# Four residual graph layers on one core: TensorE's order of score products in the attention stage

## Chip, core and metric

One core of a Trainium2 chip runs one program. The metric is the device time of one execution in microseconds. Before the change three runs took 2996.84, 2997.98 and 2998.29 us, the median is 2997.98.

## The reference

Eight graphs (batches) of 1024 nodes with 256 features pass four layers, each of the form "normalise, relu, layer, add". The layer that this change touches is the second, a masked multi-head attention:

```
h = relu(layernorm(x))
q, k, v = h Wq + bq, h Wk + bk, h Wv + bv      # 8 heads of 32
scores = (q k^T) * 32**-0.5 * (adj + adj)      # [8 heads, 1024, 1024]
attn = softmax(scores, axis=-1)
x = x + (attn v) Wo + bo
```

The others are a gated aggregation, a hypergraph convolution and an attention whose weights are adj * exp(q k^T). Everything is float32.

## The kernel before

All engines run their own instruction stream over the eight batches in turn, and are held together by semaphores alone. The order of work on each engine is written out by hand.

In the attention stage the work is cut into 64 units a batch. A unit u is one tile of 128 queries (u // 8) with one head (u % 8, through the table `ORDER`). A unit passes these steps:

- TensorE, `scores(u)` (L1271): two matmuls, 128 queries against 2 x 512 keys, into PSUM banks 0 and 1 for even units or 2 and 3 for odd ones. It first waits for `zs(b, u - 1)`, that VectorE has read the scores of unit u - 2 out of the same pair of banks.
- VectorE (L805): one pass over the 1024 scores of each row; it multiplies by the adjacency and the scale, writes `Z` and gives the maximum `nm`.
- GpSimd, `negate_max` (L565): changes the sign of the maximum.
- ScalarE (L1040): the exponential in place on `Z`, and the sum of each row.
- TensorE, `transposes(u)` (L1293): eight transposes of 128x128 in two halves, each half into one of three PSUM banks that are used in turn (banks 4 to 6). A half waits until the half three turns before has been copied out.
- ScalarE (L1030) copies the first half out of PSUM, VectorE (L760) the second; for one unit of eight ScalarE copies both.
- TensorE, `weighted_values` (L1321): once for four units, 64 small matmuls with the values.

TensorE's loop goes over steps u. Before the change a step issues, in this order: the output projection of a finished tile where it is due (u % 8 == 6), the scores of unit u + 2, the weighted values where they are due (u % 4 == 3), other projections in the first steps of a batch (`BESIDE`), the transposes of unit u, and `spread_inverses` (L1301, two transposes, u % 8 == 0). In step 0 the transposes come first.

VectorE's loop (L797 and on) has its own order in step u: the pass over the scores of unit u, then small work where it is due (`normalise`, `add_output`, the statistics of the next norm), then `evacuate(u - 2)`, the copy of the second half of unit u - 2. ScalarE's has the exponential of u, then its copies for unit u - 1. GpSimd changes the sign for unit u and then writes a part of `H` for the next layer.

Of the kernel before, what the change touches and what calls it, by code (L numbers as in the profile page):

```python
# [31 lines left out]
def build_program(nc, x_in, adj_in, adjT_in, mask_in, wqkT0, wv0, w1attn, bq1, bk1, bv1, bo1,  # L32
# [12 lines left out]
    UNITS = NT * HEADS  # L45
# [18 lines left out]
    with ctx:  # L64
# [258 lines left out]
        def group_due(u, lag):  # L323
            g, rest = divmod(u - lag, HPG)
            return g if rest == 0 and 0 <= g < NT * GROUPS else None

        def tile_due(u, lag):

            g = group_due(u, lag)
            return g // GROUPS if g is not None and g % GROUPS == GROUPS - 1 else None  # L330
# [61 lines left out]
        def rows(t):  # L392
            return slice(t * P, (t + 1) * P)

        def half(n):
            return slice(n * HALF, (n + 1) * HALF)
# [715 lines left out]
        def _(pe):  # L1112
# [43 lines left out]
            def batch(b):  # L1156
# [35 lines left out]
                def project_kq(n):  # L1192
                    s, w, g = KQ[n]
                    product(ps[:, KQ_BANK[n]], [((Wk1, Wq1)[w][:, c, rows(g)], hT1[:, c, half(s)]) for c in range(DT)]).then_inc(kq_ps.sem, 1)

                def project_v(n):

                    if n == 0:
                        pe.wait_ge(*lasts(b, 4))
                    else:  # L1200
                        pe.wait_ge(*vs(b, n))
                    if n == 2:
                        pe.wait_ge(*lo_s(b, len(KQ)))
                    for i in range(2):
                        mm = product(ps[:, 7, i * D:(i + 1) * D], [(hT1[:, c, rows(2 * n + i)], Wv1[:, c]) for c in range(DT)])
                    mm.then_inc(v_ps.sem, 1)
# [52 lines left out]
                def scores(u):  # L1259
                    t, hd = u // HEADS, ORDER[u % HEADS]  # L1260
                    if u >= 2:
                        pe.wait_ge(*zs(b, u - 1))
                    j = hd % HPG
                    if hd < HPG - 1 and t == 0:
                        for s in range(NH):
                            if j < len(kS_in[s]):
                                pe.wait_ge(*kS_in[s][j](b, 64))
                    if hd < len(qS_in[t // TPH]) and t % TPH == 0:
                        pe.wait_ge(*qS_in[t // TPH][j](b, 64))
                    for s in range(NH):  # L1270
                        mm = pe.matmul(ps[:, 2 * (u % 2) + s], qS[:, hd, rows(t)], kS[:, hd, half(s)], start=True, stop=True)  # L1271
                    mm.then_inc(S_ps.sem, 1)
# [15 lines left out]
                def transposes(u):  # L1288
                    pe.wait_ge(*exps(b, u + 1))
                    for s in range(2):  # L1290
                        wait_bank((u, s))
                        for a in range(NT // 2):
                            mm = pe.transpose(ps[:, turn_bank((u, s)), rows(a)], Z[:, u % ZS, rows(NT // 2 * s + a)], ident[:])  # L1293
                        mm.then_inc(T_ps.sem, 1)

                def spread_inverses(t):

                    pe.wait_ge(*rss(b, t + 1))
                    at, first = sums_at(t)
                    for g in range(GROUPS):  # L1300
                        mm = pe.transpose(ps[:, at, first + P * g:first + P * (g + 1)],  # L1301
                                          rs[:, HPG * g:HPG * (g + 1)].rearrange("p h d -> p (h d)"), ident[:])
                    mm.then_inc(R_ps.sem, 1)

                def weighted_values(g, part):


                    if part == 0:
                        pe.wait_ge(*PT_act(b, by_act(HPG * g + HPG - 1)))
                        pe.wait_ge(*PT_dve(b, by_dve(HPG * g + HPG - 1)))  # L1310
                        t = g // GROUPS
                        if g == 0:
                            pe.wait_ge(*vs(b, NT // 2))
                        if g % GROUPS and t < NT - 1:
                            pe.wait_ge(*Rss(b, t + 1))
                        if g % GROUPS == 0 and t:
                            pe.wait_ge(*ctxs(b, t))
                    for kt in range(sum(PARTS[:part]), sum(PARTS[:part + 1])):
                        for j in range(HPG):
                            hd = ORDER[HPG * (g % GROUPS) + j]  # L1320
                            mm = pe.matmul(ps[HD * j:HD * j + HD, 7, P * (g % GROUPS):P * (g % GROUPS + 1)],  # L1321
                                           v[:, kt, HD * hd:HD * hd + HD], PT(HPG * g + j)[:, kt],
                                           start=(kt == 0), stop=(kt == NT - 1))
                    if part == len(PARTS) - 1:
                        mm.then_inc(pv_ps.sem, 1)

                def project(t):
                    pe.wait_ge(*ctxs(b, t + 1))
                    if t < NT - 1:
                        wait_bank((t, "out"))  # L1330
                    product(ps[:, out_bank(t), 0:D], [(ctxn[:, g], Wo1[:, g]) for g in range(GROUPS)]).then_inc(o_ps.sem, 1)
# [10 lines left out]
                for u in range(STEPS):  # L1342
                    if (t := tile_due(u, PROJECT)) is not None:
                        project(t)
                    if u == 0:
                        transposes(u)
                    if u + 2 < UNITS:
                        scores(u + 2)
                    for part in range(len(PARTS)):
                        if (g := group_due(u, WEIGH + part)) is not None:  # L1350
                            weighted_values(g, part)
                    if u in BESIDE:
                        what, n = BESIDE[u]
                        if what == "v":
                            project_v(n)
                        else:
                            pe.wait_ge(*vs(b, 2))
                            project_kq(n)
                    if 0 < u < UNITS:
                        transposes(u)  # L1360
                    if (t := tile_due(u, SPREAD)) is not None:
                        spread_inverses(t)
# [137 lines left out]
            with pe.Fori(0, B) as b:  # L1500
                batch(b)
# [43 lines left out]
```

## Time and profile before

| | us |
|---|---|
| median of three runs | 2997.98 |
| profiled execution, its own time | 2997.46 |
| its span | 2995.7 |
| TensorE matmul busy | 2931.8 (98%) |
| VectorE busy | 1874.1 (63%) |
| ScalarE busy | 1491.7 (50%) |
| GpSimd busy | 722.8 (24%) |

Busy time is the time in which an engine has an instruction at work. The matmuls overlap each other in their records, so the distance between the starts of two matmuls, not the length of a record, tells what one costs. All times in the rows are counted from the start of the span. An entry in square brackets behind a row is idle time of the engine just before it, and what ended it.

### The profile page before, as it was taken

The numbers are of one execution on the slowest core, as the hardware profiler recorded it, in microseconds if no ns is written. First come the engines' busy times: TensorE is split into PE (matmuls) and PEld (weight loads), VectorE is DVE, ScalarE is ACT, GpSimd is POOL, SyncE is SP. The second block draws the span as 40 slices with busy tenths as digits, with TensorE's granted clock in tenths as the row PEclk, the third lists the DMA queues.
The fourth block names the chain that finished last, engine by engine and source line by source line (L and its number), as shares of the span: only waits on it lengthen the run. The fifth ranks groups of instructions, "written<-read, shape, count | busy, mean of one in ns | idle before, by whom it ended". The sixth has DMA issues, their size and how long they took to land.

```text
span 2995.7 us, 63670 instructions
## 1 busy us (share of the span) xinstructions
PE 2931.8 (98%) x23040; PEld 2369.1 (79%) x23040; DVE 1874.1 (63%) x4154; ACT 1491.7 (50%) x2761; POOL 722.8 (24%) x1305
## 2 busy tenths in 40 slices
PE   7999999999999999999999999999999999999999
PEld 6887788877878778888788886888868888688886
DVE  2798427974278742887428874288643886438863
ACT  1784218833178332883328732387323872238622
POOL 0343003430034201342013420134201341014410
PEclk9999999999999999999999999999999999999999
DMA  5202212022120231202311113111132022220200
GB/s 174 93 2 92 78 72 93 2 92 87 62 93 2 92 108 50 84 22 72 134 37 71 49 49 130 56 53 58 58 112 75 34 75 69 84 81 26 83 8 14
DMA packets 95320, 204.34 MB, mean 68 GB/s; under 512 B 10512, under 2 KB 41616, under 8 KB 94992
## 3 DMA queue, kind: packets, MB, share of 16 engines
q1 hardware_dynamic: 93456, 195.76, 18.0%
q8 instruction: 206, 3.38, 0.5%
q0 software_dynamic: 1536, 4.20, 0.4%
q14 instruction: 122, 1.00, 0.1%
HBM read 136.75 MB, written 8.65 MB: 49 GB/s over the span
## 4 chain that ended last, share of the span: by engine, by line
PE 70%; DVE 12%; issue 10%; POOL 4%; ACT 2%; DVEq 0%; DMA 0%; SPq 0%; POOLq 0%; ACTq 0%
PE ps L1116 40%; PE ps L1293 8%; PE ps L1371 7%; PE ps L1271 4%; PE ps L1443 4%; PE ps L1321 4%; DVE junk L847 3%; POOL H L577 3%; DVE Z L805 2%; DVE stats L628 1%; DVE h L863 1%; DVE dn L856 1%; POOL nm L565 1%; ACT Z L1040 1%; PE ps L1153 1%
## 5 line engine op out<-in xcount | busy, mean ns | idle before, releaser
L805 DVE CUSTOM_DVE_ANT_0 Z<-ps,adjN 128x1024 f32<-128x1024 f32 x512 | 623.7, 1218 | 63.7 <-PE ps L1271 63.7
L1040 ACT ACTIVATE Z<-Z,nm 128x1024 f32<-128x1024 f32 x512 | 587.4, 1147 | 51.8 <-POOL nm L565 51.8
L1293 PE MATMUL ps<-ident,Z 128*128 128x128 f32 x4096 | 546.1, 276 | 20.1 <-ACT Z L1040 17.7
L1293 PEld LDWEIGHTS ps<-ident,Z 128*128 128x128 f32 x4096 | 458.8, 140 | 130.0 <-issue 63.8
L1271 PE MATMUL ps<-kS,qS 128*128 128x512 f32 x1024 | 370.4, 444 | 0.8 <-issue 0.8
L577 POOL TENSOR_SCALAR H<-adjN 128x128 fp32r<-128x128 f32 (+1 forms) x456 | 317.5, 696 | 0.0
L565 POOL TENSOR_TENSOR nm<-nm,minus 128x1 f32<-128x1 f32 x512 | 98.1, 192 | 640.0 <-DVE nm L805 635.4
L1116 PE MATMUL ps<-mh,adjT 128*128 128x256 f32 x1024 | 223.6, 379 | 0.0
L1116 PE MATMUL ps<-v,P 128*128 128x257 f32 x1024 | 223.6, 379 | 0.0
L1116 PE MATMUL ps<-hT,t3T 128*128 128x512 f32 x512 | 221.0, 592 | 0.0
L1116 PEld LDWEIGHTS ps<-v,P 128*128 128x128 f32 x1024 | 193.8, 189 | 31.9 <-issue 3.8
L1116 PEld LDWEIGHTS ps<-mh,adjT 128*128 128x128 f32 x1024 | 193.9, 190 | 26.0
L760 DVE COPY PTa<-ps 128x512 f32<-128x512 f32 x256 | 175.8, 687 | 31.8 <-PE ps L1293 31.8
L1116 PEld LDWEIGHTS ps<-hT,t3T 128*128 128x128 f32 x512 | 97.3, 190 | 119.1 <-issue 118.6
L542 POOL TENSOR_SCALAR ve<-mv 128x4 f32<-128x4 f32 x64 | 12.7, 199 | 733.3 <-DVE mv L633 732.6
L701 DVE CUSTOM_DVE_ANT_0 E<-ps,G 128x256 f32<-128x256 f32 x64 | 27.2, 424 | 245.0 <-PE ps L1116 211.0
L1116 PE MATMUL ps<-W,hT 128*128 128x256 f32 x768 | 176.9, 380 | 0.0
L1030 ACT ACTIVATE PTb<-ps 128x512 f32<-128x512 f32 x256 | 144.3, 589 | 59.5 <-PE ps L1293 59.5
L1030 ACT ACTIVATE PTa<-ps 128x512 f32<-128x512 f32 x256 | 150.8, 589 | 38.9 <-PE ps L1293 38.9
L1271 PEld LDWEIGHTS ps<-kS,qS 128*128 128x128 f32 x1024 | 159.5, 191 | 10.6 <-issue 4.8
L1100 ACT ACTIVATE E<-ps,cj 128x512 f32<-128x512 f32 x128 | 87.9, 687 | 159.6 <-PE ps L1116 159.6
L1116 PEld LDWEIGHTS ps<-W,hT 128*128 128x128 f32 x768 | 142.5, 190 | 22.6
(179 smaller groups left out, 5708.5 us busy)
## 6 DMA issues: line engine op xcount, KB each, us to landing
adjT<-adjT_in SPq DMA_DIRECT2D x8, 4096.0 KB, 13.0
adjN<-adj_in SPq DMA_DIRECT2D x8, 4096.0 KB, 18.0
adjT<-adjT_in SPq DMA_DIRECT2D x8, 2048.0 KB, 7.9
qS<-qhi SPq DMA_DIRECT2D x112, 128.0 KB, 2.1
qS<-qlo SPq DMA_DIRECT2D x112, 128.0 KB, 2.1
adjT<-adjT_in SPq DMA_DIRECT2D x8, 1536.0 KB, 12.0
xn<-x_in SPq DMA_DIRECT2D x8, 1024.0 KB, 5.8
out<-x SPq DMA_DIRECT2D x8, 1024.0 KB, 4.8
```

The costliest lines, as they stand in the source:

```text
L565: pool.tensor_tensor(nm[:, u:u + 1], nm[:, u:u + 1], minus[:], ALU.mult).then_inc(nms.sem, 1)
L577: done = pool.tensor_scalar(H[:, t, of], adjN[:, t, of], 0.0, 0.0, ALU.is_equal, ALU.is_equal)
L760: dve.tensor_copy(PT(u)[:, NT // 2:NT], heads_of(ps[:, bank])).then_inc(PT_dve.sem, 1)
L805: dve.tensor_tensor_reduce(Z[:, u % ZS], ps[:, 2 * (u % 2):2 * (u % 2) + 2].rearrange("p a n -> p (a n)"), adjN[:, u // HEADS], SCORE_SCAL ...
L1030: act.activation(PT(u)[:, first:first + NT // 2], heads_of(ps[:, bank]), ACT.Copy).then_inc(PT_act.sem, 1)
L1040: act.activation(Z[:, u % ZS], Z[:, u % ZS], ACT.Exp, bias=nm[:, u:u + 1], accum_out=sm[:, u:u + 1]).then_inc(exps.sem, 1)
L1116: mm = pe.matmul(dst, lhsT, rhs, start=(i == 0), stop=(i == len(pairs) - 1))
L1271: mm = pe.matmul(ps[:, 2 * (u % 2) + s], qS[:, hd, rows(t)], kS[:, hd, half(s)], start=True, stop=True)
L1293: mm = pe.transpose(ps[:, turn_bank((u, s)), rows(a)], Z[:, u % ZS, rows(NT // 2 * s + a)], ident[:])
L1321: mm = pe.matmul(ps[HD * j:HD * j + HD, 7, P * (g % GROUPS):P * (g % GROUPS + 1)], v[:, kt, HD * hd:HD * hd + HD], PT(HPG * g + j)[:, kt], ...
L1371: mm = pe.matmul(dst(n, i), lhs(n, j, i), rhs(n, j, i), start=(j == 0 and i == 0), stop=(j == NT - 1 and i == 0))
L1443: mm = pe.matmul(ps[:, bank(t), 0:D], HT[:, j, rows(t)], (Vh, Vl)[i][:, j], start=(j == 0 and i == 0), stop=(j == NT - 1 and i == 0))
```

## The change

In step u the scores of unit u + 2 were issued. Now an even step issues those of u + 2 and of u + 3, and an odd step issues none. Nothing else is altered; the waits inside `scores` are the same.

```
-                    if u + 2 < UNITS:
-                        scores(u + 2)
+                    if u % 2 == 0:
+                        for ahead in (u + 2, u + 3):
+                            if ahead < UNITS:
+                                scores(ahead)
```

## Rows read from the trace of the kernel before

**Rows 1.** The page's groups: line, operation, tiles and shapes, count | busy us, mean ns | idle

```profile
L805 DVE CUSTOM_DVE_ANT_0 Z<-ps,adjN 128x1024 f32<-128x1024 f32 x512 | 623.7, 1218 | 63.7 <-PE ps L1271 63.7
```

**Rows 2.** One tile's length, busy us (PE, PEld, DVE, ACT, POOL), clock, DMA

```profile
520.45:537.05 16.60, 16.36 (x217) 13.68 (x216) 15.01 (x28) 14.18 (x27) 7.22 (x18) 1.00 0.00 1
```

**Rows 3.** TensorE's waits in the whole span: total us, how many, longest

```profile
PE ps L1293 <- ACT Z L1040: 17.7, 64, 0.5
```

**Rows 4.** Order of time, TensorE, one tile: start us, length us, engine, line

```profile
520.45 0.71 PE L1271 MATMUL ps<-kS,qS 128*128 128x512 f32 x2
...
521.00 1.03 PE L1293 MATMUL ps<-ident,Z 128*128 128x128 f32 x8
...
521.87 0.38 PE L1301 MATMUL ps<-ident,rs 128*128 128x128 f32 x2
...
522.00 0.71 PE L1271 MATMUL ps<-kS,qS 128*128 128x512 f32 x2
...
522.55 1.04 PE L1293 MATMUL ps<-ident,Z 128*128 128x128 f32 x8
...
523.34 0.71 PE L1271 MATMUL ps<-kS,qS 128*128 128x512 f32 x2
...
524.30 1.09 PE L1293 MATMUL ps<-ident,Z 128*128 128x128 f32 x8 [0.24 <-ACT Z L1040]
...
525.14 0.71 PE L1271 MATMUL ps<-kS,qS 128*128 128x512 f32 x2
...
527.67 1.09 PE L1293 MATMUL ps<-ident,Z 128*128 128x128 f32 x8
...
531.34 1.13 PE L1116 MATMUL ps<-Wo,ctxn 128*128 128x256 f32 x4
...
532.12 0.82 PE L1271 MATMUL ps<-kS,qS 128*128 128x512 f32 x2
...
532.78 1.13 PE L1293 MATMUL ps<-ident,Z 128*128 128x128 f32 x8
...
533.67 0.72 PE L1271 MATMUL ps<-kS,qS 128*128 128x512 f32 x2
```

**Rows 5.** Order of time, other engines, same tile

```profile
521.38 1.23 DVE L805 CUSTOM_DVE_ANT_0 Z<-ps,adjN 128x1024 f32<-128x1024 f32 x1
...
522.53 0.68 DVE L760 COPY PTa<-ps 128x512 f32<-128x512 f32 x1
...
522.70 0.19 POOL L565 TENSOR_TENSOR nm<-nm,minus 128x1 f32<-128x1 f32 x1 [1.83 <-DVE nm L805]
...
523.14 1.21 DVE L805 CUSTOM_DVE_ANT_0 Z<-ps,adjN 128x1024 f32<-128x1024 f32 x1
...
523.98 0.19 ACT L1040 ACTIVATION_READ_ACCUMULATOR Z<-Z,nm 128x1 f32 x1
...
528.80 0.69 DVE L760 COPY PTa<-ps 128x512 f32<-128x512 f32 x1 [0.57 <-PE ps L1293]
```

**Rows 6.** Order of time, TensorE, first tile of a batch

```profile
464.30 1.03 PE L1271 MATMUL ps<-kS,qS 128*128 128x512 f32 x2
...
467.69 1.19 PE L1271 MATMUL ps<-kS,qS 128*128 128x512 f32 x4
...
468.72 1.89 PE L1116 MATMUL ps<-W,hT 128*128 128x256 f32 x8
...
481.76 0.71 PE L1271 MATMUL ps<-kS,qS 128*128 128x512 f32 x2
...
483.02 1.09 PE L1293 MATMUL ps<-ident,Z 128*128 128x128 f32 x8 [0.55 <-ACT Z L1040]
...
483.87 0.71 PE L1271 MATMUL ps<-kS,qS 128*128 128x512 f32 x2
```

**Rows 7.** Order of time, end of the stage: a product that waits for VectorE

```profile
606.10 0.41 DVE L773 TENSOR_TENSOR ctxn<-ps,Rs 128x256 f32<-128x256 f32 x1
...
606.56 1.13 PE L1116 MATMUL ps<-Wo,ctxn 128*128 128x256 f32 x4 [0.60 <-DVE ctxn L773]
```

## The prediction

> **What bounds the kernel now.** I read the costliest groups first [rows 1]: the largest of all is VectorE's pass over the scores (L805), so the diff touches the largest stage, attention. Then the busy times of one tile of that stage, eight units [rows 2]. It takes 16.60 us; TensorE is busy 16.36, VectorE 15.01, ScalarE 14.18, GpSimd 7.22. So TensorE sets the pace, but VectorE is only a tenth behind: an order that makes TensorE wait for VectorE at the wrong place has little to give back. The granted clock is 1.00 there. Third, the waits by pairs [rows 3]: the only regular wait of TensorE in the loop is that of the transposes for the exponential, 64 times (8 a batch), 17.7 us in all. Fourth, the order of time of one tile [rows 4] and of the other engines beside it [rows 5]. There the loop can be followed: scores, VectorE, GpSimd's sign, ScalarE's exponential, transposes.
>
> I number the units of a tile 0 to 7 (u mod 8) and write S2 for the two score matmuls of unit 2, z2 for VectorE's pass over them, T2 for its eight transposes, c0 for VectorE's copy of half of T0. Step s is where Ts is issued. In the tile of [rows 4], S2 stands at 520.45, T0 at 521.00, the two small transposes of `spread_inverses` at 521.87, S3 at 522.00, T1 at 522.55, S4 at 523.34, T2 at 524.30, S5 at 525.14. The group of weighted values (W) follows in steps 3 and 7, the output projection in step 6.
>
> Prices on TensorE, start to start [rows 4]: S then T 0.55; T then S 0.79 (522.55 to 523.34); T then another transpose 0.87 (521.00 to 521.87); `spread_inverses` then S 0.13. T2 should follow S4 after 0.55, at 523.89, and starts at 524.30: 0.41 late. It then takes 0.84 instead of 0.79 to the next S, so waiting costs 0.05 more: 0.46 a tile. T6 starts on time (532.78 after S at 532.12; the pair behind the projection takes 0.66 in place of 0.55) but takes 0.89 instead of 0.79, 0.10 more, since it meets ScalarE's two late copies. These are the stalls a reordering can win.
>
> **The change, part by part.** No instruction is added or removed; no DMA, VectorE, ScalarE or GpSimd queue is changed. Each S with an odd number is issued one step earlier: S3 before T0, S5 before T2, S7 before T4, S9 before T6. It is moved past one T, past `spread_inverses` in step 0, and with S9 past the place between projection and W. Four cases.
>
> (a) The matmuls by themselves. At the start of a batch two units stand in a row already: from 467.69 the four score matmuls take until 468.72, 1.03 for two units [rows 6]. So S S T T costs 1.03 + 0.87 + 0.79 = 2.69 where S T S T costs 2 x (0.55 + 0.79) = 2.68. Nothing is gained or lost. Where the order beside W changes, S T S W becomes S S T W with the same kinds of border; I take 0, and 0.05 a tile to either side for the range.
>
> (b) The wait that is removed. S5 now stands between S4 and T2 and fills T2's wait: 0.46 less a tile, if S5 itself is free to go. T6 gets S9 ahead of it and comes 0.55 later than the copies it waited for: 0.10 less.
>
> (c) The wait that is added. S(n) must wait until z(n-2) has read the bank pair. S3 needs z1, S5 needs z3, S7 needs z5, S9 needs z7. Behind the waiting S5, TensorE holds T2, W and T3, which are ready; nothing else on it may pass. Its new time is built from S2 = 0:
> T0 at 1.03; `spread_inverses` at 1.90; T1 at 1.90 + 0.13 + 0.08 (the difference of 0.87 and 0.79, a transpose follows and no S) = 2.11; S4 at 2.90; S5 could start at 3.45 and T2 at 2.90 + 1.03 = 3.93.
> VectorE: z2 starts 0.93 after S2 (520.45 to 521.38) [rows 4, 5]. c0 comes 1.15 after z2, at 2.08, but has to have T0, whose record ends 1.03 after its start, and 0.04 for the hand-over (527.67 + 1.09 = 528.76, copy at 528.80): 1.03 + 1.03 + 0.04 = 2.10. z3 starts 0.61 after c0 (522.53 to 523.14), at 2.71. GpSimd, which is released by the same instruction, starts 1.32 after z does (521.38 to 522.70) [rows 5]. From the end of z (1.23) TensorE needs 0.05 if it behaves as it does for `ctxn` (606.51 to 606.56) [rows 7], or 0.13 as for the exponential (524.17 to 524.30) [rows 4, 5]. The ends are 1.28 and 1.36; I take 1.32, the row of the same releaser. S5 then starts at 2.71 + 1.32 = 4.03, 0.58 after it could. The pair behind the projection costs 0.66 to the next T; a pair behind a wait lacks a weight load ahead of time in the same way, so I take 0.66. T2 starts at 4.69 in place of 3.93: 0.76 more a tile. Bounds: 0.55 for the pair and 1.28 give T2 at 4.54, 0.61 more. The slowest pair of the trace has a record of 1.03 where the usual one has 0.71 (464.30 [rows 6] and 520.45 [rows 4]), so 0.87 to the next; with 1.36 that gives 4.94, 1.01 more.
>
> The Trainium skill (TensorE: Matmul & The Clock Gate, Part 2, "Step-by-step: what each phase is for") says that TensorE's queue pulls weight loads ahead of matmuls in flight. If it also pulled S5's load past the wait, the pair would take 0.55 and not 0.66, which takes 0.11 x 56 = 6 us off the sum below. The transposes that waited speak against it: T2 took 0.05 longer behind its wait [rows 4].
>
> (d) The other moved pairs. By the same steps (T's end 1.07 after its start, a copy 0.61, z to S 1.32) S(n) can go 3.00 after the start of the T whose copy stands ahead of z(n-2). S7: 3.00 after T2. Between stand T2 (0.87), W (525.14 to 527.67 less 0.55 for S, 1.98), T3 (0.79) and S6 (0.55), 4.19 in all; free. S9: 3.00 after T4. Between stand T4 and T5 (0.87 each), the projection (531.34 to 532.12, 0.78) and S8 (0.66), 3.18; free by 0.18. S11, the S3 of the next tile: z9 stands behind c6 as well, W and T7 lie between; free. z2 is not held up: T7 starts 0.79 before S2, so c7 can start at 1.07 - 0.79 = 0.28 and is through at 0.89, before z2 at 0.93.
>
> The first tile of a batch is different. In step 0 the old order already has S2, S3 in a row [rows 6]. In step 2 other projections lie beside the loop and no stall arises. In step 6, T6 waits for the exponential until 483.02, then come S9 at 483.87 and W. S8 starts at 481.76, S9 then fits between 482.31 and 483.02: 0.50 less a batch. In step 62, at the end of the batch, there is no S left to put ahead of T62, so nothing is won there.
>
> Sum for a batch: seven tiles lose 0.76 (5.32), seven win 0.46 (3.22), six win 0.10 (0.60), the first tile wins 0.50. 5.32 - 3.22 - 0.60 - 0.50 = +1.00; eight batches +8 us. The profiled execution took 2997.46 (its span is 2995.7), so it goes to 3005.5; from the median of the runs, 2997.98, to 3006.0.
>
> **Rivals.**
> 1. No measurable change. The new wait is at its lower bound, 0.61: 4.27 - 4.32 = -0.05 a batch, 0 in all; up to 0.72 it stays below 0.2%. For it: all terms are differences of a few hundredths, and the one restart of a matmul behind VectorE took only 0.05 [rows 7]. Against it: it needs both the short wake and a pair that restarts without loss. Time 2998 to 3004.
> 2. Faster. The mechanism would be that S5 finds z3 done: then the stalls in (b) are pure gain, -4.32 x 8 = -35 us, 2963. The point from which it decides: z3 has to start 0.58 earlier, which is nearly the 0.61 of c0, the copy between z2 and z3. If VectorE were ahead by one such copy, it would hold. Against it: VectorE's queue is fixed, and both c0 and z3 itself (it writes the `Z` buffer that T0 reads) need T0 to be through. For a win of 6 us the new wait would have to cost below 0.51 a tile, which is under both bounds.
> 3. Clearly slower. The restart costs as much as the pair at 464.30, 1.01 a tile: 7.07 - 4.32 = 2.75, +22 us, 3020. It gets there too if S9 in step 6 waits: its spare 0.18 is small, and 0.2 of waiting in seven tiles and eight batches is 11 us on top of the forecast. For it also: VectorE has only 1.6 us of slack in a tile.
> 4. The change has no effect because the second pair waits until the old place. For S5 it comes close: the old order issues it after T2 (525.14, 4.69 after S2), the new one at 4.03. T2, which once went ahead of it, would then go behind it. If S5 got no earlier than 4.69, T2 would come at 5.35, 1.42 a tile: 9.94 - 4.32 = 5.62 a batch, +45 us, 3043. Against it: the steps of (c) leave nothing for S5 to wait for after 4.03.
>
> **How the numbers follow.** A difference of 0.2% is 6 us, about what can be told from none. Forecast 0.42; rival 1 0.32; rival 2 0.08; rival 3 0.16; rival 4 0.02. The likeliest is the forecast. Slower by over 0.2% has the forecast and rival 3, 0.60 together; the forecast's 8 us lies close to the 6, and 0.06 of it may fall below. So slower 0.54, same 0.38, faster 0.08. Low end: 0 with 0.05 x 56 = 3 us for the borders of (a), 2995. High end: +22 with 3, 3023.
>
> **What would show it.** In the changed profile the pairs of L1271 stand in fours. S5 starts about 4.0 after S2, with an idle or late start released by VectorE's L805, 56 such waits. T2 no longer waits for ScalarE; the regular wait of L1293 for the exponential shrinks from 64 to the first tiles' 8. Tiles take 16.60 + 0.76 - 0.46 - 0.10 = 16.80. All other stages keep their length. The prediction is wrong if S5 does not wait, if S9 or S3 waits, if the tile is under 16.60, or if T1 or T5, which now stand straight behind T0 and T4, wait for the copies of the PSUM banks.

## The result, and the profile after

The changed kernel takes 3015.0 us (median of four runs, 3013.99 to 3016.09), the kernel before 2997.9 in the same comparison: a ratio of 1.0058, 95% interval 1.0045 to 1.0071. That is 17.1 us slower, inside the range of 2995 to 3023 and on the forecast side, but twice the forecast 8.

The page of the changed kernel, busy times first, then the groups that answer to [rows 1] and the matmuls of the loop (busy, mean of one, idle before and what ended it):

```profile
PE 2933.7 (97%) x23040; PEld 2388.5 (79%) x23040; DVE 1883.9 (63%) x4154; ACT 1509.6 (50%) x2761; POOL 722.8 (24%) x1305
...
L805 DVE CUSTOM_DVE_ANT_0 Z<-ps,adjN 128x1024 f32<-128x1024 f32 x512 | 624.0, 1219 | 59.7 <-PE ps L1271 59.7
...
L1293 PE MATMUL ps<-ident,Z 128*128 128x128 f32 x4096 | 535.1, 275 | 3.0 <-ACT PTb L1030 2.3
...
L1271 PE MATMUL ps<-kS,qS 128*128 128x512 f32 x1024 | 328.2, 431 | 31.7 <-DVE nm L805 31.7
```

VectorE's pass is as long as before (1219 ns a piece). The idle time of the transposes for ScalarE, 17.7 us in [rows 3], is gone from their line; the scores have 31.7 us in its place, released by VectorE. The waits of TensorE say how often:

```profile
PE ps L1271 <- DVE nm L805: 31.7, 64, 0.9
```

64 waits for VectorE stand where 64 waits for ScalarE stood. The prediction had 56, one in each tile but the first. So each batch has one more. It is the long one, of 0.9 us: without it (the first experiment below, where the first tile has the old order) 56 waits of together 24.5 us are left.

One tile of the changed kernel, columns as in [rows 2]:

```profile
508.32:525.07 16.75, 16.31 (x218) 14.05 (x216) 15.20 (x28) 14.48 (x27) 7.21 (x18) 1.00 0.01 3
```

The tile went from 16.60 to 16.75 us; 16.80 was forecast. The sum over a batch then shows where the time is. All lengths are medians over the eight batches of one profiled execution. I take the first tile from S0 to T7's start and the others from the last transpose of a tile to that of the next. The first tile went from 24.46 to 25.42, +0.96 (in the batch whose rows are shown, from 461.94 to 486.40 before and from 465.27 to 490.69 after). Tiles 1 to 6 went from 16.60 to 16.76, +0.16 each. The last went from 16.13 to 16.38, +0.25. The rest of a batch takes 228.52 in both. Together 0.96 + 0.96 + 0.25 = 2.17 a batch, 17.4 us in eight. Single batches differ (one of the eight first tiles of the kernel before took 25.41), and the spans of the two profiled executions are 16.7 us apart. The loss of the later tiles is as forecast; the first tile, which was to win 0.50, lost 0.96.

The changed tile in order of time, the rows that answer to [rows 4, 5]. S2 starts at 508.32:

```profile
508.32 1.17 PE L1271 MATMUL ps<-kS,qS 128*128 128x512 f32 x4
...
509.25 1.23 DVE L805 CUSTOM_DVE_ANT_0 Z<-ps,adjN 128x1024 f32<-128x1024 f32 x1
509.33 1.03 PE L1293 MATMUL ps<-ident,Z 128*128 128x128 f32 x8
...
510.42 1.04 PE L1293 MATMUL ps<-ident,Z 128*128 128x128 f32 x8
510.49 0.69 DVE L760 COPY PTa<-ps 128x512 f32<-128x512 f32 x1
510.57 0.19 POOL L565 TENSOR_TENSOR nm<-nm,minus 128x1 f32<-128x1 f32 x1 [1.74 <-DVE nm L805]
...
511.10 1.22 DVE L805 CUSTOM_DVE_ANT_0 Z<-ps,adjN 128x1024 f32<-128x1024 f32 x1
...
511.21 0.72 PE L1271 MATMUL ps<-kS,qS 128*128 128x512 f32 x2
...
512.37 0.73 PE L1271 MATMUL ps<-kS,qS 128*128 128x512 f32 x2 [0.44 <-DVE nm L805]
...
512.94 1.03 PE L1293 MATMUL ps<-ident,Z 128*128 128x128 f32 x8
...
516.64 1.19 PE L1271 MATMUL ps<-kS,qS 128*128 128x512 f32 x4
...
517.67 2.02 PE L1293 MATMUL ps<-ident,Z 128*128 128x128 f32 x16
...
519.53 1.09 PE L1116 MATMUL ps<-Wo,ctxn 128*128 128x256 f32 x4
...
520.27 1.03 PE L1271 MATMUL ps<-kS,qS 128*128 128x512 f32 x3
```

S2 and S3 stand in one group, T0 follows at 1.01 (forecast 1.03), T1 at 2.10 (2.11), S4 at 2.89 (2.90). z2 is at 0.93. The copy c0 comes at 2.17 (2.10) and z3 at 2.78 (2.71). c0 has to have T0, whose record ends at 1.01 + 1.03 = 2.04; the copy starts 0.13 behind that end, where the forecast had 0.04. S5 starts at 512.37, 4.05 after S2 (4.03), and 1.27 after z3: a wait of 1.16 - 0.55 = 0.61 behind S4. T2 follows S5 after only 0.57 (0.66), at 4.62 (4.69), and does not wait for ScalarE.

In the row at 520.27 (S8 and S9) the fourth matmul lies outside the window of this view.

The new wait in the first tile of a batch. This is the stretch from the end of step 2 to T4:

```profile
476.07 1.14 ACT L1040 ACTIVATE Z<-Z,nm 128x1024 f32<-128x1024 f32 x1
...
477.49 0.69 ACT L990 ACTIVATE qhi<-ps,bq1c 128x512 fp32r<-128x512 f32 x1 [0.18 <-PE ps L1116]
...
478.21 0.75 DVE L745 SCALAR_TENSOR_TENSOR qlo<-ps,bq1c,qhi 128x512 fp32r<-128x512 f32 x1 [1.49 <-ACT qhi L990]
...
478.88 0.68 DVE L760 COPY PTa<-ps 128x512 f32<-128x512 f32 x1
...
479.13 0.71 PE L1271 MATMUL ps<-kS,qS 128*128 128x512 f32 x2
479.48 1.22 DVE L805 CUSTOM_DVE_ANT_0 Z<-ps,adjN 128x1024 f32<-128x1024 f32 x1
...
480.75 0.30 PEld L1271 LDWEIGHTS ps<-kS,qS 128*128 128x128 f32 x2 [1.34 <-DVE nm L805]
480.75 0.73 PE L1271 MATMUL ps<-kS,qS 128*128 128x512 f32 x2 [0.91 <-DVE nm L805]
...
481.32 1.89 PE L1116 MATMUL ps<-W,hT 128*128 128x256 f32 x8
...
483.04 1.04 PE L1293 MATMUL ps<-ident,Z 128*128 128x128 f32 x8
```

The projection of step 2 is followed by ScalarE's `qhi` (L990) and by VectorE's `lower_kq` (L745) that reads it. `qhi` stands behind an exponential, but that was over when it started; its row names the projection (L1116) as what it waited for. Behind `lower_kq` on VectorE stand c2 and z5. So z5 starts at 479.48, when S6 has already been issued, and S7 can start only 1.27 later, at 480.75, 1.62 after S6 instead of 0.55. Behind S7 TensorE holds the projection of the values at 481.32 and T4 at 483.04.

The same stretch of the kernel before:

```profile
474.60 0.75 DVE L745 SCALAR_TENSOR_TENSOR qlo<-ps,bq1c,qhi 128x512 fp32r<-128x512 f32 x1 [1.20 <-ACT qhi L990]
...
475.63 0.71 PE L1271 MATMUL ps<-kS,qS 128*128 128x512 f32 x2
...
475.86 1.22 DVE L805 CUSTOM_DVE_ANT_0 Z<-ps,adjN 128x1024 f32<-128x1024 f32 x1
```

There too z5 starts behind S6, 0.23 after it, but S7 was issued only after T4, at 478.70, and had nothing to wait for.

### The profile page after: what moved, and what is told of

Its sections match the earlier page's. It is cut to its first block, busy times and chain, and to the rows that moved or that the text cites. A ratio compares the mean times of both kernels' runs of the same rounds, so it can differ in the third digit from the quotient of the medians.

```text
span 3012.4 us, 63670 instructions
## 1 busy us (share of the span) xinstructions
PE 2933.7 (97%) x23040; PEld 2388.5 (79%) x23040; DVE 1883.9 (63%) x4154; ACT 1509.6 (50%) x2761; POOL 722.8 (24%) x1305
## 4 chain that ended last, share of the span: by engine, by line
PE 80%; DVE 11%; issue 5%; ACT 2%; POOL 1%; DVEq 0%; DMA 0%; SPq 0%; POOLq 0%; ACTq 0%
PE ps L1116 40%; PE ps L1293 13%; PE ps L1271 7%; PE ps L1373 7%; PE ps L1321 7%; PE ps L1445 4%; DVE junk L847 3%; DVE stats L628 1%; DVE h L863 1%; DVE dn L856 1%; POOL H L577 1%; PE ps L1153 1%; DVE Z L805 1%; DVE Ul L688 1%; ACT h2T L1072 1%
## 5 line engine op out<-in xcount | busy, mean ns | idle before, releaser
L805 DVE CUSTOM_DVE_ANT_0 Z<-ps,adjN 128x1024 f32<-128x1024 f32 x512 | 624.0, 1219 | 59.7 <-PE ps L1271 59.7
L1293 PE MATMUL ps<-ident,Z 128*128 128x128 f32 x4096 | 535.1, 275 | 3.0 <-ACT PTb L1030 2.3
L1271 PE MATMUL ps<-kS,qS 128*128 128x512 f32 x1024 | 328.2, 431 | 31.7 <-DVE nm L805 31.7
L1271 PEld LDWEIGHTS ps<-kS,qS 128*128 128x128 f32 x1024 | 171.9, 189 | 85.2 <-DVE nm L805 59.7
L1116 PE MATMUL ps<-mh,adjT 128*128 128x256 f32 x1024 | 223.6, 379 | 0.0
L1116 PE MATMUL ps<-v,P 128*128 128x257 f32 x1024 | 223.6, 379 | 0.0
L1116 PE MATMUL ps<-hT,t3T 128*128 128x512 f32 x512 | 221.0, 592 | 0.0
L1116 PEld LDWEIGHTS ps<-v,P 128*128 128x128 f32 x1024 | 193.8, 189 | 31.9 <-issue 3.8
L1116 PEld LDWEIGHTS ps<-mh,adjT 128*128 128x128 f32 x1024 | 193.9, 190 | 26.0
L1116 PEld LDWEIGHTS ps<-hT,t3T 128*128 128x128 f32 x512 | 97.3, 190 | 119.1 <-issue 118.6
L1116 PE MATMUL ps<-W,hT 128*128 128x256 f32 x768 | 177.6, 381 | 0.0
L934 DVE TENSOR_TENSOR P<-E,adjT 128x512 f32<-128x512 f32 x128 | 88.7, 693 | 113.6 <-ACT E L1100 113.6
## 6 DMA issues: line engine op xcount, KB each, us to landing
adjN<-adj_in SPq DMA_DIRECT2D x8, 4096.0 KB, 17.1
```

Source lines behind the costliest of these rows:

```text
L805: dve.tensor_tensor_reduce(Z[:, u % ZS], ps[:, 2 * (u % 2):2 * (u % 2) + 2].rearrange("p a n -> p (a n)"), adjN[:, u // HEADS], SCORE_SCAL ...
L1116: mm = pe.matmul(dst, lhsT, rhs, start=(i == 0), stop=(i == len(pairs) - 1))
```

## The experiments

All are changes of the list of units that a step issues, or of the one constant `BOTH`. Times are medians; the kernel before took 2998.2 us beside the first four, 2996.8 beside the next four and 2997.0 beside the last two. Lengths of tiles are again medians over one profiled execution; "the tile" is one of tiles 1 to 6 of a batch, counted from 0.

**Which tiles lose.** First the old order in the first tile alone, then pairs in the first tile alone.

```
+ for ahead in ((u + 2,) if u < HEADS else ((u + 2, u + 3) if u % 2 == 0 else ())):
```

> Pairs only from step 8 of a batch on; the first tile (steps 0 to 7) keeps the old order. Theory A (the changed kernel's loss is 1.0 us in the first tile and 0.15 us in every later one, because in the first tile S7 waits for z5, which stands behind lower_kq on VectorE): the first tile returns to 19.55 us and the time falls by 8 x 1.0 = 8 us to about 3007, later tiles stay at 16.75. Rival B (the first tile's loss only moves: the wait is met by the next pair): under 3 us gained, 3012 or more.

Measured: 3008.3 us (ratio 1.0035, 1.0021 to 1.0048). The first tile is back at its length of before, later tiles are at 16.76.

```
+ for ahead in (((u + 2, u + 3) if u % 2 == 0 else ()) if u < HEADS else (u + 2,)):
```

> Pairs only in steps 0 to 7 of a batch, the old order in all later tiles. Theory A: first tile 20.5 us, later tiles 16.60 as before the change, time 2998 + 8 = 3006. Rival B: what is lost in the first tile is won back by TensorE's waits behind it, time 2998 to 3001.

Measured: 3004.9 us (1.0023, 1.0014 to 1.0032). The first tile is 0.96 longer than before, all later ones 16.60. So the two losses stand beside each other and add: 10.1 us of the later tiles and 6.7 of the first make 16.8, against 17.1 for the change. Rival B fell in both.

**What fails in the first tile.** One unit is put back, S7:

```
+ for ahead in ((u + 2,) if u in (4, 5) else ((u + 2, u + 3) if u % 2 == 0 else ())):
```

> The changed kernel with one unit put back: the scores of unit 7 are issued in step 5 again, behind T4, all other pairs stay. Theory A: S7's wait is the whole fault of the first tile; without it the first tile is 0.5 us shorter than the old 19.55 (the gain that the prediction had for step 6), so 1.5 us a batch and 12 us in all are won, 3003. Rival C (pairing in the first tile is bad in several places, S5 or S9 too): the first tile stays over 19.8 us and the time over 3008.

Measured: 3005.2 us (1.0023, 1.0014 to 1.0033), ten less than the change. The first tile is 1.28 shorter than with the change and 0.31 shorter than the old one (463.99 to 488.14 from S0 to T7, 24.15 against 24.46). The rows from S6 on:

```profile
477.85 0.71 PE L1271 MATMUL ps<-kS,qS 128*128 128x512 f32 x2
...
478.19 1.22 DVE L805 CUSTOM_DVE_ANT_0 Z<-ps,adjN 128x1024 f32<-128x1024 f32 x1
...
478.40 1.89 PE L1116 MATMUL ps<-W,hT 128*128 128x256 f32 x8
...
480.12 1.04 PE L1293 MATMUL ps<-ident,Z 128*128 128x128 f32 x8
...
480.91 0.71 PE L1271 MATMUL ps<-kS,qS 128*128 128x512 f32 x2
```

z5 is as late as before, 0.34 after S6. But TensorE does the projection (478.40) and T4 (480.12) in the meantime, and S7 at 480.91 finds z5 long done. So S7's place is the fault of the first tile: it costs 1.28, of which 1.07 is the distance of 1.62 from S6 in place of 0.55. Rival C fell by its numbers. Of the 0.50 that the prediction gave to step 6, 0.31 is left over the whole tile. The pair of step 6 itself wins 0.48 (from S8 to T7 4.64 before, 4.16 now). Steps 2 and 3 lose 0.18 (from S4 to S6 4.39 before, 4.57 now), in this run and in the changed kernel alike: the second half of T3 starts 0.56 behind the first and not 0.44, since it needs the PSUM bank that ScalarE's copy of T2's first half frees, and this copy now stands behind `qhi`. That `lower_kq` is what makes z5 late is read from the rows; no run moved it.

**The later tiles, taken apart.** Pairs in step 2 alone, and pairs everywhere but in step 2:

```
+ for ahead in ((u + 2,) if u < HEADS or u % HEADS not in (2, 3) else ((u + 2, u + 3) if u % 2 == 0 else ())):
```

> Old order everywhere but in step 2 of each tile from the second on (u % 8 == 2), where S4 and S5 stand together: S5's wait for z3 alone. Theory A: S5's wait costs 0.69 a tile and takes away T2's 0.46, so tiles are 16.60 + 0.23 = 16.83 and seven tiles in eight batches lose 13 us, 3011. Rival D (T2's late start is kept as well, since nothing is filled): 16.60 + 0.69 = 17.29, 3037.

Measured: 3006.8 us (1.0030, 1.0018 to 1.0041), tile 16.76. The loss is smaller than the 0.23 expected, and rival D's 17.29 fell. The same stretch as above:

```profile
507.20 0.71 PE L1271 MATMUL ps<-kS,qS 128*128 128x512 f32 x2
...
508.14 1.23 DVE L805 CUSTOM_DVE_ANT_0 Z<-ps,adjN 128x1024 f32<-128x1024 f32 x1
...
509.29 0.69 DVE L760 COPY PTa<-ps 128x512 f32<-128x512 f32 x1
...
509.89 1.22 DVE L805 CUSTOM_DVE_ANT_0 Z<-ps,adjN 128x1024 f32<-128x1024 f32 x1
...
511.17 0.73 PE L1271 MATMUL ps<-kS,qS 128*128 128x512 f32 x2 [0.36 <-DVE nm L805]
```

S5 starts 3.97 after S2 here, 0.08 earlier than with all pairs. c0 comes 1.15 after z2, not 1.24: with S3 behind T0, T0 is 0.46 earlier and c0 doesn't wait for it.

```
+ for ahead in ((u + 2,) if u < HEADS or u % HEADS in (2, 3) else ((u + 2, u + 3) if u % 2 == 0 else ())):
```

> Pairs in steps 0, 4 and 6 of each tile from the second on; step 2 keeps the old order (S5 behind T2), and so does the first tile. Theory A: no new wait and T2's old one; T6's 0.10 is won and the second half of T5, which now waits for a bank, costs 0.05 to 0.1: tiles 16.55 to 16.60, time 2994 to 2998. Rival E (pairs cost TensorE something by themselves, at the borders T to T and S to S): tiles over 16.65 and 3001 or more.

Measured: 2992.7 us (0.9986, 0.9977 to 0.9995), tile 16.49. It is 4.1 us faster than the kernel before, and the tile is shorter than the 16.55 to 16.60 expected; rival E fell. The pairs of steps 0, 4 and 6 win 0.11 a tile, all of it behind S8 (from there to T7 4.08 before, 3.96 now). The pair of step 2 loses 0.16 by itself and 16.76 - 16.49 = 0.27 beside the others: with S3 ahead of T0, c0 comes later and S5 waits 0.09 longer.

**Is c0 what S5 waits for?** `BOTH = 0` lets ScalarE copy both halves of unit 0, so that VectorE has no c0 between z2 and z3, and gets c5 instead. First with the old order, to see what this costs by itself:

```
-    BOTH = 5
+    BOTH = 0
```

> The kernel before with BOTH = 0 in place of 5: ScalarE copies both halves of unit 0 of each tile, VectorE both none of it, and unit 5 is shared as usual. Theory A: in the old order VectorE's copy c0 is no bound, T2 still waits for the exponential; T6's 0.10 goes, T0's neighbours get it. Tile 16.5 to 16.7, time 2990 to 3004. Rival F (the copy c0 delays z3 and with it the old order too): tile 16.3 or less, 2980.

Measured: 3019.3 us (1.0075, 1.0062 to 1.0089), tile 16.93. Both expectations missed. The rows around T6 show why:

```profile
517.12 1.22 DVE L805 CUSTOM_DVE_ANT_0 Z<-ps,adjN 128x1024 f32<-128x1024 f32 x1
...
518.43 0.42 DVE L780 TENSOR_TENSOR x<-ps,x 128x256 f32<-128x256 f32 x1
...
518.70 0.65 PE L1293 MATMUL ps<-ident,Z 128*128 128x128 f32 x4
518.77 0.68 DVE L760 COPY PTb<-ps 128x512 f32<-128x512 f32 x1
...
519.51 0.65 PE L1293 MATMUL ps<-ident,Z 128*128 128x128 f32 x4 [0.16 <-DVE PTb L760]
```

T6's first four transposes start at 518.70, the other four at 519.51, 0.81 later and not 0.49 as in the kernel before; that is the 0.33 by which the tile is longer. They need the bank of T5's second half. Its copy, now VectorE's, stands behind z7 and `add_output` and ends at 519.45.

Then with the order of the changed kernel:

```
-    BOTH = 5
+    BOTH = 0      # and pairs in every even step
```

> The changed kernel with BOTH = 0: VectorE has no copy c0 between z2 and z3, so z3 starts when T0 is through, 2.10 after S2 and not 2.71. Theory A (S5 waits because c0 stands ahead of z3): S5 may go 3.4 after S2, when TensorE is there, the wait of 0.61 goes and T2 follows without one; tile 16.75 - 0.65 = 16.1, time 3015 - 36 = 2979, less than the kernel before. Rival G (VectorE as a whole is the bound of the paired order, so that c5, now on VectorE, makes another S wait): tile 16.6 or more, 3006 or more.

Measured: 2992.2 us (0.9985, 0.9976 to 0.9994), tile 16.26. `BOTH = 0` costs the old order 22 us (against the kernel before) and gives the paired order about as much (17.1 us slower without it, 4.6 us faster with it). Rival G fell. S5's wait is nearly gone. The tile around T2:

```profile
504.41 1.17 PE L1271 MATMUL ps<-kS,qS 128*128 128x512 f32 x4
...
505.35 1.23 DVE L805 CUSTOM_DVE_ANT_0 Z<-ps,adjN 128x1024 f32<-128x1024 f32 x1
...
506.13 1.08 ACT L1030 ACTIVATE PTa<-ps 128x512 f32<-128x512 f32 x2 [0.15 <-PE ps L1293]
...
506.65 1.23 DVE L805 CUSTOM_DVE_ANT_0 Z<-ps,adjN 128x1024 f32<-128x1024 f32 x1
...
507.11 1.15 ACT L1040 ACTIVATE Z<-Z,nm 128x1024 f32<-128x1024 f32 x1
...
507.30 1.37 PE L1271 MATMUL ps<-kS,qS 128*128 128x512 f32 x4
...
507.94 0.30 PEld L1271 LDWEIGHTS ps<-kS,qS 128*128 128x128 f32 x2 [0.36 <-DVE nm L805]
...
508.51 1.06 PE L1293 MATMUL ps<-ident,Z 128*128 128x128 f32 x8
```

z3 starts 1.30 after z2 (505.35 to 506.65) and not 1.85. That is 0.20 behind the end of T0's record (505.42 + 1.03). In the first tile of this run, where T0 is long through, z3 follows z2 after 1.15; so here it still waits for T0, but for 0.15 only. S5 (its weight loads are at 507.94) follows S4 (507.30) after 0.64 in place of 1.16. Theory A holds for the mechanism; the size was less, 22 to 23 us of the 36 expected. Tiles 1 to 6 gained 0.50 and not 0.65. z3 comes 2.24 after S2, not 2.10. And T2, at 508.51, comes 1.40 after the start of its exponential (507.11). A T2 that waits for it comes 1.37 after (509.09 to 510.46 in the last run below). ScalarE's two copies of unit 0 (506.13) have pushed that exponential back, so T2 could go hardly any earlier. The rest lies outside these tiles: the last tile gained 0.15 (16.38 to 16.23), and the rest of a batch took 0.37 longer (228.52 to 228.89). Why the latter is so was not followed up. T6's trouble of the previous run is covered, as S9 stands ahead of it.

And with the old order in the first tile:

```
+ for ahead in ((u + 2,) if u < HEADS else ((u + 2, u + 3) if u % 2 == 0 else ())):     # and BOTH = 0
```

> As the one before, BOTH = 0 with pairs, but only from step 8 of a batch on. Theory A: the two effects add, 1.0 us a batch less than with pairs from the start, 2979 - 8 = 2971. Rival H: the first tile's loss depends on who copies unit 0 and the difference is under 3 us.

Measured: 2983.8 us (0.9958, 0.9945 to 0.9972), 8.4 less than the run before it. That difference is theory A's 8, and rival H fell; the time itself, 2971, was missed, as it stood on the 2979 of the run before.

```
+ for ahead in ((u + 2,) if u in (4, 5) else ((u + 2, u + 3) if u % 2 == 0 else ())):     # and BOTH = 0
```

> BOTH = 0, pairs in every even step, but in the first tile the scores of unit 7 stay behind T4 (step 5). Theory A (the first tile loses by S7's wait alone and wins 0.31 us by its other pairs, as it did with BOTH = 5): first tile 0.3 us shorter than with the old order there, 2.4 us in all, 2981. Rival H (with BOTH = 0 the first tile's waits are others): no difference from 2984, or more.

Measured: 2982.3 us (0.9950, 0.9936 to 0.9964). The first tile is 0.29 shorter than in the run before it. The difference of the two times, 1.5 us, is too small to be told from none by the times alone. It is the fastest kernel of this study, 15 us faster than the kernel before.

The last one has the old order in the first tile, and takes the pair of step 2 out as well:

```
+ for ahead in ((u + 2,) if u < HEADS or u % HEADS in (2, 3) else ((u + 2, u + 3) if u % 2 == 0 else ())):     # and BOTH = 0
```

> BOTH = 0, pairs in steps 0, 4 and 6 from the second tile on, step 2 and the first tile in the old order. Theory A: with c0 off VectorE, standing S5 before T2 wins 0.24 a tile (S4 to T2's end 2.20 against 2.44 us) where with c0 it lost 0.25. So without the pair in step 2 the tile is 16.26 + 0.24 = 16.50 and the time 2984 + 13 = 2997. Rival I (the gain of BOTH = 0 is not S5's but comes from elsewhere): tile 16.26 to 16.35, under 2989.

Measured: 3009.4 us (1.0044, 1.0030 to 1.0058), tile 16.71. Rival I fell. The direction is theory A's, the size nearly twice: the pair of step 2 wins 0.45 a tile and not 0.24. The wait that it fills has grown, as the rows show:

```profile
509.09 1.15 ACT L1040 ACTIVATE Z<-Z,nm 128x1024 f32<-128x1024 f32 x1
...
509.29 0.72 PE L1271 MATMUL ps<-kS,qS 128*128 128x512 f32 x2
...
510.46 0.76 PE L1293 MATMUL ps<-ident,Z 128*128 128x128 f32 x5 [0.45 <-ACT Z L1040]
```

T2 starts 1.17 after S4 (before: 0.96), waiting for the exponential, which stands behind ScalarE's two copies of unit 0. The copies alone don't do this: with `BOTH = 0` in the old order T2 came 0.96 after S4. It takes the pair of step 0 as well, which puts T0, and so its copies, 0.46 later. With S5 ahead of T2 that time is used.

The tiles of the four kernels with the old first tile:

| tile, us | step 2 in the old order | S4 and S5 as a pair |
|---|---|---|
| c0 on VectorE (`BOTH = 5`) | 16.49 | 16.76 |
| c0 on ScalarE (`BOTH = 0`) | 16.71 | 16.26 |

The same pair costs 0.27 or wins 0.45, 0.72 apart. The larger part is the copy between z2 and z3: with the pair, S5 starts 4.06 after S2 where the copy stands there and 3.53 where it doesn't. The smaller part, 0.21, is the exponential's wait that the pair fills, which is longer with `BOTH = 0` (T2 without the pair at 4.06 after S2 and not 3.85).

## Why the prediction was right, and where not

The direction and the mechanism of the later tiles were right. That 3015.0 still lies in the range is in part luck: the upper end, 3023, was set for a slow restart of the waiting pair, which did not happen, and not for what did.

- **(a) The matmuls by themselves: right.** Steps 0 and 1 take 2.89 in both kernels, from S2 to S4 (520.45 to 523.34, and 508.32 to 511.21).
- **(b) The waits removed: right.** T2 no longer waits. From S8 to W, the stretch around T6 took 0.66 + 0.89 + 0.65 = 2.20 and takes 2.08 after, 0.12 less where 0.10 was forecast.
- **(c) The wait added: right in place and mechanism.** T2 comes at 4.62, 0.69 late, where 0.76 was forecast. z3 was 0.07 later than forecast, because c0 came 0.13 behind T0's end and not 0.04; the step from z3 to S5 took 1.27 and not 1.32; and the pair behind the wait took 0.57 and not 0.66. The last is the term with the largest error: the row behind the projection was the wrong one to take it from, the usual 0.55 was nearly right. The reason given for 0.66, a weight load that is not ahead of time, does not hold for that row either: the first load of the pair behind the projection starts 0.02 before its matmul (532.10 and 532.12), that of a usual pair 0.03 (520.42 and 520.45).
  The Trainium skill (TensorE: Matmul & The Clock Gate, Part 2, "Step-by-step: what each phase is for") says that the queue pulls weight loads ahead of matmuls in flight. The prediction asked whether it also pulls one past a wait, which would give 0.55. The time is near that, but the load was not pulled: the weight load of the waiting S7 starts at 480.75, at the same time as its matmul. A waiting pair loses only 0.02 all the same.
- **(d) The other moved pairs in later tiles: right.** S3, S7 and S9 do not wait. One thing that the prediction named as a sign of being wrong came in small: T5's second half waits for ScalarE's copy to free its PSUM bank, and starts 0.49 behind the first and not 0.44. The output projection follows T4 after 1.86 where two transposes in a row cost 1.74; 0.05 of this is that wait.
- **The first tile: wrong, and this is the miss.** The step that failed is "in step 2 other projections lie beside the loop and no stall arises", together with (d), which checked S7 with the prices of a later tile. The projection of step 2 is not only work on TensorE: it puts `lower_kq` into VectorE's queue ahead of z5, after a wait for ScalarE. With the step written out, S7's wait could be seen from code and rows of before: z5 at 475.86 and 1.27 more is 477.13, and a pair behind S6 could go at 475.63 + 0.55 = 476.18. S7's place costs 1.28 a batch. The forecast for step 6 was nearly right, 0.48 for 0.50, but the late second half of T3 takes 0.18 away, so that the rest of the first tile won about 0.31. Against the forecast the first tile is 0.96 + 0.50 = 1.46 a batch or 11.7 us worse, and the later tiles are 1.50 - 1.21 = 0.29 a batch or 2.3 us better. The balance is 9.4 by these medians, and the measurement is 9.1 above the forecast of 8.
- **Rivals.** Rival 2 named its point of decision: z3 has to come earlier by about one copy. The runs with `BOTH = 0` took that copy away, and the paired order then won, though not only by it (see the table). Rival 3 was near in time (3020), for another reason: neither the restart nor S9 in step 6, but S7 in step 4 of the first tile. Rivals 1 and 4 fell.

## What to carry to other kernels

An instruction that is moved up in an in-order queue brings its wait with it, and everything behind it then waits too. Follow the releaser's own queue to the instruction just ahead of the one that releases: here one copy of 0.61 us was the larger part of what made the same reordering lose 0.27 or win 0.45 us a tile. Write the timetable out for each kind of iteration, the first one with its extra work too, since a steady tile says nothing of it. And try a reordering together with the constant that shares work between engines: here all pairs alone made the kernel 17.1 us slower and `BOTH = 0` alone 22, both together 4.6 us faster.

## What the runs showed that was not expected

- A pair of score matmuls that waited for VectorE follows at once: 0.57 us to the next transpose against 0.55 without a wait. Transposes that waited cost 0.05 more, and the pair behind the output projection 0.11 more.
- From the start of VectorE's pass to the matmul that waits for it 1.27 us go by, 0.05 of them after the end of the pass (1.22). A transpose that waits for ScalarE starts 0.13 after the end of the accumulator's read [rows 4, 5]. So the hand-over is not the same in these two rows. Nor is it from TensorE to VectorE: a copy for which VectorE stood idle starts 0.04 after the end of the transposes' record [rows 4, 5], c0 right behind a pass 0.13, and z3 right behind a pass 0.20.
- Small moves add up exactly only where their stretches do not touch. The first tile and the later ones add (6.7 + 10.1 against 17.1 us); pairs of one tile don't (+0.16 and -0.11 make +0.16), mostly because S3's place sets when c0 can start: S5 waits 0.09 longer.
